# A post-norm decoder layer on one core: one set of f16 halves and paired matmuls for cross attention, an f16 ffn turned by DMA, one wide rotary product, new engine orders

## What is computed

```
x = layernorm(x + attn(x, Wqkv, q_norm_w, k_norm_w, Wo))  # 16 heads of 32; rmsnorm and rope on q and k; causal
x = layernorm(x + xattn(x, ctx, ctx))                     # 8 heads of 16 tokens each; attention between features
x = layernorm(x + ffn(x, weight))                         # quant_dequant(x) @ quant_dequant(weight).T

def xattn(q, k, v):                # q.reshape(b * 8, 16, 512), k and v likewise
    sm = softmax(einsum('bdm,bdn->bmn', q, k) / 4)        # 512 x 512 per head, sum over the 16 tokens of the head
    return einsum('bmn,bcn->bcm', sm, v)

def quant_dequant(x):              # per block of 128: s = max|x| / 448, round x / s to fp8 e4m3, times s
```

## Time and profile before

| | |
|---|---|
| runs, us | 2977.68, 2983.88, 2977.72; median 2977.72 |
| profiled execution: span, us | 2976.2 (its own time is not listed apart from the three runs) |
| busy: PE, DVE, ACT, POOL | 2769.9 (93%), 2635.4 (89%), 1875.6 (63%), 1390.6 (47%) |
| DMA moved, share of 16 engines | 463.95 MB, 57% |
| first and last slot | the first batch's second step on DVE starts at 68.3 us, the last batch's at 2757.2 us |

### The profile page before, as it was taken

The page is one execution under the profiler, slowest core; times in us unless marked ns, Lnnn a source line. Parts: engine busy times, 40 slices in busy tenths (PEclk is TensorE's granted clock), DMA queues, the critical chain, the costliest instruction groups (busy, mean ns, idle before and its releaser), DMA issues.

```text
span 2976.2 us, 70796 instructions
## 1 busy us (share of the span) xinstructions
PE 2769.9 (93%) x19216; PEld 1384.5 (47%) x19216; DVE 2635.4 (89%) x4035; ACT 1875.6 (63%) x3521; POOL 1390.6 (47%) x1879
## 2 busy tenths in 40 slices
PE   1679999999999999999999999999999999999986
PEld 1444445445444544544454454445444544544422
DVE  6259999999999999999999999999999999999874
ACT  0236676666667666666766666676667666666654
POOL 2334554454455445445544544554455445445421
PEclk9789999999999999999999999999999999999987
DMA  2256666665566556555655666565566656555640
GB/s 81 59 156 156 161 175 164 155 177 164 160 161 178 164 157 170 167 165 153 181 166 154 168 172 166 151 182 163 155 168 174 166 155 174 165 164 155 171 133 29
DMA packets 647619, 463.95 MB, mean 156 GB/s; under 512 B 350720, under 2 KB 580096, under 8 KB 647424
## 3 DMA queue, kind: packets, MB, share of 16 engines
q1 hardware_dynamic: 647424, 462.07, 57.1%
HBM read 208.68 MB, written 186.12 MB: 133 GB/s over the span
## 4 chain that ended last, share of the span: by engine, by line
PE 42%; DVE 37%; issue 18%; POOL 1%; DMA 1%; DVEq 1%; ACT 1%; SPq 0%; POOLq 0%; ACTq 0%
DVE nm L754 12%; PE pv L1035 11%; PE bank L911 10%; PE st L1023 6%; PE mx L1009 6%; DVE ropeA L793 3%; DVE o2t L834 3%; PE bank L904 2%; DVE sh L761 2%; PE bank L947 2%; PE bank L950 2%; DVE ropeB L797 2%; DVE ropeB L795 2%; DVE st L818 1%; DVE yc L845 1%
## 5 line engine op out<-in xcount | busy, mean ns | idle before, releaser
L614 ACT ACTIVATE pp<-st 128x512 f32<-128x512 f32 x2048 | 1163.4, 596 | 720.6 <-PE st L1023 449.1
L754 DVE TENSOR_REDUCE nm<-mx 128x2 f32<-128x1024 f32 x1024 | 1243.8, 1215 | 79.0 <-PE mx L1009 78.3
L1023 PE MATMUL st<-qst,kst 98*128 98x512 f16 x2048 | 734.2, 389 | 7.5 <-ACT pp L614 4.5
L1035 PE MATMUL pv<-pp,vT 128*32 128x512 f32 x4096 | 525.2, 608 | 0.0
L1009 PE MATMUL mx<-kpair,qpair 64*128 64x512 bf16 x2048 | 403.0, 390 | 55.2 <-DVE nm L754 48.4
L911 PE MATMUL bank<-w_h,xT_h 128*128 128x512 f32 x768 | 399.1, 520 | 7.3 <-DVE xT_l L785 7.3
L1023 PEld LDWEIGHTS st<-qst,kst 98*128 98x128 bf16 x2048 | 175.6, 97 | 422.6 <-ACT pp L614 209.9
L595 POOL TENSOR_TENSOR qpl<-x,qpl 128x512 f16<-128x512 f32 x64 | 74.2, 1160 | 581.0 <-ACT qpl L667 581.0
L1009 PEld LDWEIGHTS mx<-kpair,qpair 64*128 64x128 f16 x2048 | 98.4, 93 | 528.4 <-DVE nm L754 321.3
L911 PE MATMUL bank<-w_l,xT_h 128*128 128x512 f32 x768 | 306.5, 399 | 0.0
L911 PE MATMUL bank<-w_h,xT_l 128*128 128x512 f32 x768 | 306.2, 399 | 0.0
(11 more groups left out here) (124 smaller groups left out, 4786.4 us busy)
## 6 DMA issues: line engine op xcount, KB each, us to landing
qst<-q_rows SPq DMA_DIRECT2D x128, 320.0 KB, 4.4
kst<-k_rows SPq DMA_DIRECT2D x128, 320.0 KB, 4.3
qpair<-q_pair_rows SPq DMA_DIRECT2D x256, 128.0 KB, 2.6
kpair<-k_pair_rows SPq DMA_DIRECT2D x256, 128.0 KB, 2.7
q_pair_rows<-qpl SPq DMA_DIRECT2D x64, 384.0 KB, 2.9
q_rows<-qpl SPq DMA_DIRECT2D x64, 384.0 KB, 3.1
k_pair_rows<-kpl SPq DMA_DIRECT2D x64, 384.0 KB, 2.4
k_rows<-kpl SPq DMA_DIRECT2D x64, 384.0 KB, 2.7
```

The lines of the kernel that those rows point to most:

```text
L614: a.activation(pp[:, unit % 2, j, :], st[n % 2][:], ACT.Exp, scale=CROSS_SCALE).then_inc(st_free, 1)
L754: v.tensor_reduce(cols, mx[:], AX.X, ALU.max, negate=True).then_inc(mx_free, 1)
L1023: t.matmul(st[n % 2][:], kst[:, h, i * P:(i + 1) * P], qst[:, h, :], start=True, stop=True).then_inc(st_full, 1)
L1035: last = t.matmul(pv[32 * j:32 * j + 2 * XD, :], vT[b.i][:, i, GROUPS * j + g, :], pp[:, unit % 2, j, :], start=(i == 0), stop=(i == KC - 1))
```

## The change

Cross attention keeps one set of rows for both products. The context is scaled by a power of two found from its sum of squares (`ctx_square`, a store and a broadcast load of 128 numbers, `ctx_total`, `ctx_pow`, `ctx_exp`, `ctx_scale`), and split in two f16 halves instead of three bf16 parts (`context_high`, `context_low`). Query and context go to DRAM once each in three copies of parts, and come back as 24 rows per head, two heads side by side, into `qp` and `kp`, of which there are now two buffers each. `cross_scores_T` is paired like `cross_scores`: 16 pairs of matmuls of 26 rows into the two banks of `st`, and one `probs` of 128x1024 for each pair, whose scale is now an operand (`esc`, undoing the power of two, `ctx_inv`). There is one `cross_shift` of 32 columns for all heads in place of two of 16, with one store and four one-row loads. The multiply of `cross_norm` goes to POOL (`cross_scale`), the rest is `cross_turn`. The rotary product is one DVE instruction of 128x1024 in place of three, and `rope_sum` is two POOL instructions of half the size. The ffn's input is split on ACT and POOL in f16 halves (`xd_high`, `xd_low`), turned by one DMA transpose (`turn_xd`), and multiplied as f16 with weights kept as two f16 parts, scaled by a power of two; `add_ffn` undoes that. `quant_T`, `xdT_high` and `xdT_low` are gone, and so are `st_kpair`, `st_qpair`, the loads of `kst` and `qst`, and 6 of the 9 copies that were stored of each. The setup reads the ffn weights first and finds their maximum over all partitions by way of DRAM. All five lists are new, and there is one more stage (0 to 8), so 72 slots.

```diff
--- before.py
+++ after.py
-        cos_w = [sb(f"cos_w{i}", [P, NH, 2, HH]) for i in range(2)]
-        sin_w = [sb(f"sin_w{i}", [P, NH, 2, HH]) for i in range(2)]
+        wf_h, wf_l = sb("wf_h", [P, KC, D], F16), sb("wf_l", [P, KC, D], F16)
+        rope_w = [sb(f"rope_w{i}", [P, 2, NH, 2, HH]) for i in range(2)]
...
+        qp = [sb(f"qp{i}", [P, PAIRS, D], F16) for i in range(2)]
+        kp = [sb(f"kp{i}", [P, PAIRS, D], F16) for i in range(2)]
...
-        st = [bank(f"st{i}") for i in range(2)]
+        st = es.enter_context(nc.psum_tensor("st", [P, 2, 512], F32))
...
         DVE_STEPS = steps("""
+            self_norm:0@2 cross_max:6@4 quant_scale:0@7 cross_max:7@4 quant_magic:0@7 cross_max:8@4
+            add_self:0@2 cross_max:9@4 self_max:0@1 self_max:1@1 cross_max:10@4 xT_low:0@0
+            ctx_exp:0@3 self_max:2@1 cross_max:11@4 cross_turn:0@5 cross_max:12@4 self_max:3@1
+            cross_max:13@4 self_shift:0@1 cross_max:14@4 rope_terms:0@0 cross_max:15@4 add_ffn:0@7
+            cross_shift:0@4 cross_max:0@3 add_cross:0@6 cross_max:1@3 rope_terms:1@0 cross_max:2@3
+            cross_max:3@3 ctx_inv:0@3 cross_max:4@3 cross_turn:1@5 cross_max:5@3 self_recip:0@1""")
         PE_STEPS = steps("""
+            proj_v:0@1 proj_v:1@1 self_scores_T:1@2 cross_scores_T:15@6 cross_scores:2@4 proj_v:2@1
+            proj_v:3@1 self_scores_T:2@2 cross_scores_T:0@5 cross_scores:3@4 self_pv:0@2 self_pv:1@2
+            cross_scores_T:1@5 cross_scores:4@4 cross_pv:7@6 self_scores_T:3@2 cross_scores_T:2@5
+            cross_scores:5@4 self_pv:2@2 self_pv:3@2 cross_pv:0@5 cross_scores_T:3@5 context_T:0@4
+            cross_scores:6@4 cross_scores_T:4@5 cross_pv:1@5 cross_scores:7@4 cross_scores_T:5@5
+            proj_o:0@2 proj_o:1@2 cross_scores:8@4 proj_o:2@2 proj_o:3@2 cross_scores_T:6@5
+            cross_pv:2@5 cross_scores:9@4 cross_scores_T:7@5 self_scores:0@1 self_scores:1@1
+            self_scores:2@1 cross_scores:10@4 cross_scores_T:8@5 x_T:0@0 self_scores:3@1 cross_pv:3@5
+            cross_scores:11@4 proj_q:0@0 proj_q:1@0 cross_scores_T:9@5 cross_scores:12@4 proj_q:2@0
+            proj_q:3@0 cross_scores_T:10@5 cross_scores:13@4 cross_pv:4@5 ffn:0@7 cross_scores:14@4
+            cross_scores_T:11@5 ffn:1@7 ffn:2@7 cross_scores:15@4 cross_scores_T:12@5 ffn:3@7
+            proj_k:0@0 proj_k:1@0 proj_k:2@0 cross_scores:0@3 cross_scores_T:13@5 proj_k:3@0
+            self_scores_T:0@1 cross_pv:5@5 cross_pv:6@5 cross_scores:1@3 cross_scores_T:14@5""")
...
         ACT_STEPS = steps("""
+            value:0@1 probs:0@5 self_probs:2@2 probs:1@5 self_probs:3@2 probs:2@5 layernorm:1@7
+            part_high:1@1 probs:3@5 oT_high:0@2 probs:4@5 context_out:0@4 ctx_square:0@3 probs:5@5
+            probs:6@5 probs:7@5 ctx_total:0@3 xd_high:0@7 xT_high:0@0 probs:8@5 context_high:0@3
+            probs:9@5 layernorm:0@2 layernorm:2@8 probs:10@5 square:0@0 probs:11@5 probs:12@5
+            probs:13@5 part_high:0@0 square:1@0 self_probs:0@1 probs:14@5 query_high:0@2
+            self_probs:1@1 probs:15@5""")
...
             def st_kpl(b, _):
+                sp.dma_start(kpl_d[b.idx()][:, 0:2, :], kpl[:]).then_inc(d_kpl_stored, 16)
+                sp.dma_start(kpl_d[b.idx()][:, 2, :], kpl[:, 0, :]).then_inc(d_kpl_stored, 16)
...
+            def ld_kp(b, g):
+                sp.wait_ge(d_kpl_stored, b.n(32, 32))
+                sp.sem_inc(passed_sp, 1)
+                sp.wait_ge(st_full, b.n(N_ST, N_ST // GROUPS * (g + 1) - 2 * N_ST))
...
+                    sp.dma_start(kp[b.i][ROW_TILE * q:ROW_TILE * q + XROWS, PG * g:PG * (g + 1), :],
+                                 kpl_d[b.idx()].rearrange("(l q g d) r n -> g q (d r) l n", q=2, g=GROUPS, d=XD)[g][q])\
+                      .then_inc(d_kp[g], 16)
...
+            def turn_xd(b, _):
+                sp.wait_ge(s_xdl, b.n(1, 1))
+                sp.sem_inc(passed_sp, 1)
+                sp.wait_ge(*full("ffn", b, -1))
+                sp.sem_inc(passed_sp, 1)
+                sp.dma_start_transpose(xdT[:], xd[:].rearrange("p a d -> p (a d)")).then_inc(d_xdT, 16)
...
-                g_.tensor_tensor(ropeA[:], ropeA[:], ropeB[:], ALU.add).then_inc(s_rope, 1)
+                g_.tensor_tensor(rope[:, 0, :, 0, :], rope[:, 0, :, 0, :], rope[:, 1, :, 1, :], ALU.add)
+                g_.tensor_tensor(rope[:, 0, :, 1, :], rope[:, 0, :, 1, :], rope[:, 1, :, 0, :], ALU.add).then_inc(s_rope, 1)
...
+            def ctx_pow(b, _):
+                pool.wait_ge(s_ctot, b.n(1, 1))
+                pool.sem_inc(passed_pool, 1)
+                pool.wait_ge(s_sc, b.n(1, 0))
+                pool.sem_inc(passed_pool, 1)
+                g_.tensor_scalar(cpow[:], ctot[:], 2.0 ** (-2 * CTX_BITS), TINY, ALU.mult, ALU.add).then_inc(s_cadd, 1)
+                pool.wait_ge(s_cadd, b.n(1, 1))
+                g_.tensor_tensor(cpow[:], cpow[:], half[:], ALU.pow).then_inc(s_cpow, 1)
+            def ctx_scale(b, _):
+                pool.wait_ge(s_sc, b.n(1, 1))
+                pool.sem_inc(passed_pool, 1)
+                g_.tensor_scalar(cxs[:], cx[:], sc[b.i][:], 1.0, ALU.mult, ALU.mult).then_inc(s_cxs, 1)
+            def context_low(b, _):
+                pool.wait_ge(s_cxs, b.n(1, 1))
+                pool.sem_inc(passed_pool, 1)
+                pool.wait_ge(s_kh, b.n(1, 1))
+                g_.tensor_tensor(kpl[:, 1, :], cxs[:], kpl[:, 0, :], ALU.subtract).then_inc(s_kl, 1)
...
+            def xd_low(b, _):
+                pool.wait_ge(s_xdh, b.n(1, 1))
+                g_.tensor_tensor(xd[:, 1, :], yq[:], xd[:, 0, :], ALU.subtract).then_inc(s_xdl, 1)
+            def cross_scale(b, g):
+                pool.wait_ge(s_o2b, b.n(1, 0))
+                pool.sem_inc(passed_pool, 1)
+                pool.wait_ge(s_r2, b.n(GROUPS, g + 1))
+                g_.tensor_tensor(o2n[:, :, g, :], o2t[g][:, :, 0:XD],
+                                 r2[:, g].unsqueeze(2).to_broadcast([P, D // 32, XD]), ALU.mult).then_inc(s_o2n, 1)
...
-                a.activation(pp[:, unit % 2, j, :], st[n % 2][:], ACT.Exp, scale=CROSS_SCALE).then_inc(st_free, 1)
+                a.activation(pp[:, unit % 2, 2 * l:2 * (l + 1), :], st[:], ACT.Exp, scale=esc[b.i][:])\
+                 .then_inc(st_free, 1)
...
+                a.activation(junkc[:], cx[:], ACT.Square, accum_out=css[:]).then_inc(s_css, 1)
...
+                a.activation(junkt[:], csb[:], ACT.Copy, accum_out=ctot[:]).then_inc(s_ctot, 1)
...
+            def context_high(b, _):
+                act.wait_ge(s_sc, b.n(1, 1))
+                act.wait_ge(d_kpl_stored, b.n(32, 0))
+                a.activation(kpl[:, 0, :], cx[:], ACT.Copy, scale=sc[b.i][:]).then_inc(s_kh, 1)
...
+            def xd_high(b, _):
+                act.wait_ge(d_xdT, b.n(16, 0))
+                act.wait_ge(s_back, b.n(1, 1))
+                a.activation(xd[:, 0, :], yq[:], ACT.Copy).then_inc(s_xdh, 1)
...
+            def ctx_exp(b, _):
+                dve.wait_ge(s_cpow, b.n(1, 1))
+                dve.wait_ge(s_kl, b.n(1, -1))
+                v.tensor_scalar(sc[b.i][:].bitcast(I32), cpow[:].bitcast(I32), EXP_BITS, None, ALU.bitwise_and)\
+                 .then_inc(s_sc, 1)
+            def ctx_inv(b, _):
+                dve.wait_ge(s_sc, b.n(1, 1))
+                dve.wait_ge(st_free, b.n(N_ST, -N_ST))
+                v.tensor_scalar(esc[b.i][:].bitcast(I32), sc[b.i][:].bitcast(I32), -1.0,
+                                float((2 * ONE_BITS - 2) * 2 ** 23), ALU.mult, ALU.add).then_inc(s_esc, 1)
...
+                v.scalar_tensor_tensor(rope[:].rearrange("p t h a d -> p t (h a d)"),
+                                       at("qk"[k])[:].unsqueeze(1).to_broadcast([P, 2, D]), rms[:, k:k + 1],
+                                       rope_w[k][:].rearrange("p t h a d -> p t (h a d)"),
                                        ALU.mult, ALU.mult).then_inc(bank_free[BANK["qk"[k]]], 1)
...
+            def cross_turn(b, g):
+                dve.wait_ge(s_o2n, b.n(GROUPS, g + 1 - GROUPS))
                 dve.wait_ge(pv_unit, b.n(UNITS, KC * (g + 1)))
-                v.transpose(o2t[:].rearrange("p u i -> p (u i)"), pv[:]).then_inc(pv_free, 1)
+                v.transpose(o2t[g][:].rearrange("p u i -> p (u i)"), pv[:]).then_inc(pv_free, 1)
                 dve.wait_ge(pv_free, b.n(GROUPS, g + 1))
-                v.reciprocal(r2[:, g].unsqueeze(2), o2t[:, :, XD:XD + 1]).then_inc(s_r2, 1)
-                dve.wait_ge(s_r2, b.n(GROUPS, g + 1))
-                dve.wait_ge(*full("xdT", b, -1))
-                v.tensor_tensor(o2n[:, :, g, :], o2t[:, :, 0:XD],
-                                r2[:, g].unsqueeze(2).to_broadcast([P, D // 32, XD]), ALU.mult).then_inc(s_o2n, 1)
+                v.reciprocal(r2[:, g].unsqueeze(2), o2t[g][:, :, XD:XD + 1]).then_inc(s_r2, 1)
...
-                v.tensor_tensor(xdT_l[:], at("xdT")[:], xdT_h[:].bitcast(F32), ALU.subtract)\
...
```

(65 more changed lines are left out.)

356 lines of the change are left out of this document (149 added, 207 removed).

## The result

The changed kernel takes 3422.55 us (median of 4 runs, 3414.28 to 3425.18) against 2978.36: a ratio of 1.148, 95% interval 1.147 to 1.150. It is slower, and 19% over the top of the range.

What follows compares the result with a forecast made beforehand. DVE was taken to bound the kernel, with PE close behind. 67.25 slots each losing 3.94 us gave 2976.2 - 265 + 18 (new stage) + 4 (setup) = 2733, median 2735 us; range 2640 to 2870.

Steps and rivals of the forecast that it cites:

- the "DMA" term of the sum: DMA transfers: 3 of 9 query and context copies each stay, `turn_xd` adds half a 4.4 us transpose; cost nothing.
- Rival E: PE's list in lock step: late `probs` delays `mx`, DVE sits out PE's turns; slot 44.4 us, 3080 us; chance 0.04.
- A: Rival: the waits nearly vanish and nothing holds DVE; slot 38.1 us, 2655 us; chance 0.17.
- B: Rival: POOL holds three small or two-input DVE instructions by 0.8 us; slot 41.3 us, 2870 us; chance 0.12.
- C: Rival: the score ring on ACT, with `st` now one buffer; slot 41.1 us, 2856 us; chance 0.10.
- D: Rival: the new score pairs on PE don't overlap; slot 42.6 us with idle, 2957 us; chance 0.05.
- DVE's sum: DVE's own work per slot, with hand-overs and one hold by POOL: from 42.2 down to 38.05 us.
- The one longer instruction that I put down to POOL: On DVE: one hold by POOL per slot, 0.4 us added, bounds 0 and 4.0.
- The waits: DVE's waits for PE per slot: 1.25 us, up from 1.03, making the slot 39.3 us.
- PE's prices: On PE: 0.22 us per matmul pair, 0.10 per change of layout; work per slot from 41.3 to 37.1 us.
- ACT's price: On ACT: 1.1 us for each of 16 exponentials of 1024 columns with the scale as operand, bounds 0.6 and 1.2.
- The edges: Outside the steady slots: 18 us for the added stage, bounds 5 and 39, and 4 for setup, bounds 0 and 10.

Runs made afterwards that it cites:

- the kernel with both repairs: The changed kernel with the row store, and with `ctx_total` and the steps that hang on it moved later in their lists: 2897.81 us, 0.972 of before.
- the row store: The changed kernel with the sums turned by DVE into four rows of 32, stored as 128 bytes per partition: 3038.55 us, 1.020 of before.
- without the power of two: The changed kernel without the context's scaling: steps `ctx_square` to `ctx_inv` and the sums' store and load removed, context split unscaled: 2811.09 us, 0.943 of before.

## Why the prediction was wrong, point by point

- **The step that failed is the "DMA" term of the sum.** It counted the copies that go and `turn_xd` that comes. The store of the sums and their broadcast load stood in the description of the change and were given no price, neither in transfer nor in what stands behind `ctx_total` on ACT: the term stood at nothing, without a reason, and cost 8.3 us per slot (49.59 less the 41.30 of the kernel with both repairs). No row before shows a packed 4-byte store, so a bound was due: the nearest, the shift store with 64 bytes per partition, lands in 1.5 us, and the load of shift rows in 2.0. Even at these prices the round trip stands ahead of `xT_high`; with the row store ACT's wait was 3.4 us per slot, enough to end slower than before (1.020). The other 5.9 us per slot (49.59 less 43.66) come from the packed form, which no row of before could show.
- **What the store should have had** is a lower bound, the shift store's 1.5 us, and a rival of its own, since no row of before gave an upper one. The Trainium skill (DMA: Bandwidth & Descriptors, "Specifications") says that transfers under 512 bytes are done by read-modify-write, which points to this question; it gives no cost and says nothing of neighbours. If that alone made the time, the 4 bytes at a distance of 512 would be as slow as the packed ones. They land in 1.6 us for 8.5, so here small writes were slow only side by side.
- **Rival E foretold slower by another mechanism**, PE's turn of `mx` laid bare. The waits of DVE for `mx` are 2.3 us per slot in the changed kernel (90.8 us in 40 slots); not the cause. A, B, C and D gave other times; none happened. Of the seven instructions that B named, one is longer beside POOL's work (next point); those of `cross_shift` take 0.15 and 0.19 us, `ctx_exp` and `ctx_inv` 0.14.
- **DVE's sum was right.** 38.05 us with the power of two; measured, slot less waits for other engines, 37.3 without it (39.94 - 2.60; forecast 37.65, without the 0.4 of `ctx_exp` and `ctx_inv`) and 38.4 with it and its turn (41.30 less 139 us in 48 slots). The rotary product takes 1.19 us from start to start, for my 1.14. The one longer instruction that I put down to POOL is there: the residual's addition takes 1.14 us on average without the power of two and 1.19 in the changed kernel, instead of 0.69, the shortest in both runs; that POOL is the cause was not tested apart. The waits were undersized: 2.6 us per slot for the 1.25 forecast.
- **PE's prices held where rows show them.** A `mx` pair starts 0.23 us behind a `st` pair, and what follows, in another layout, 0.31 behind that, as the rows below show (kernel without the power of two). So neighbours share one change of layout, and the new pairs overlap; D falls. The sum of 37.1 as a whole was not measured, since the ends of matmuls are modelled.

```profile
1500.60 0.39 PE L1038 MATMUL st<-qp,kp 50*128 50x512 f16 x2
1500.83 0.38 PE L1024 MATMUL mx<-kp,qp 48*128 48x512 f16 x2
1501.14 0.43 PE L993 MATMUL bank<-p,va 128*32 128x128 f32 x8
```

- **ACT's price was right**: 1.11 us with the scale as an operand, 1.02 without, so 0.09 for the operand, in the changed kernel and in the one without the power of two:

```profile
L612 ACT ACTIVATE pp<-st,esc 128x1024 f32<-128x1024 f32 x1024 | 1137.5, 1111 | 580.9 <-PE st L1042 575.5
```

```profile
L608 ACT ACTIVATE pp<-st 128x1024 f32<-128x1024 f32 x726 | 742.4, 1023 | 442.0 <-PE st L1038 435.4
```

The Trainium skill (ScalarE: Activation LUTs, the section "What ACT_TABLE_LOAD costs") gives 186 ns and 0.833 per column, and about 93 more for an operand. An estimate worked out from it is 1.13 us with the operand and 1.04 without; the two rows, 1.11 and 1.02, agree within 2%.

- **The edges** were undersized: the first `xT_low` comes at 75.1 us for 68.3 (+7, forecast +4), and from the last one to the end are 254 us without the power of two and 261 with it moved, for 219 (+35 to +42, forecast 18).

The sum of 2735 is so a forecast for a kernel whose sums cost nothing on the way. Without the power of two it measured 2811, inside the stated range; with the power of two well placed 2898, still above its top of 2870. Besides the failed step the working was too low by the waits and the edges.

## What to carry to other kernels

Price every new DMA, however small, by its landing time and by what is issued behind it; a store of one number per partition should leave as rows or with its elements apart (1.8 and 1.6 us here, for 8.5 to 9.1). A round trip over DRAM belongs behind everything on its engine that does not need it. When a stall has two causes that lie on each other, undo both before judging either.
